# Two attentions of one program: scratch rows kept by head, fewer and later loads, another order at the second one's entry

## The reference, cut to what matters

```
x = ln(x + attention0(x))   # 16 heads of 8, softmax(q k / sqrt(8) - |i - j|), causal
x = ln(x + experts(x))      # 8 experts, each token to the one of its largest logit
x = ln(x + attention1(x))   # 16 heads of 64, rms norm on q and k, bias -(i - j) * omega * softplus(k . u), causal
x = ln(x + ffn(x))          # five linear maps of 128 to 512 to 512 to 512 to 128 with gates
```

## Time and profile before

| | us |
|---|---|
| median of 3 runs | 2205.83 |
| lowest, highest | 2204.8, 2212.89 |
| profiled execution | 2213.37 |
| its span, first to last instruction | 2211.6 |
| TensorE busy | 2041.5 (92%) |
| VectorE busy | 1389.9 (63%) |
| ScalarE busy | 1146.0 (52%) |

### The profile page before, as it was taken

The page is one execution under the profiler, slowest core; times in us unless marked ns, Lnnn a source line. Parts: engine busy times, 40 slices in busy tenths (PEclk is TensorE's granted clock), DMA queues, the critical chain, the costliest instruction groups (busy, mean ns, idle before and its releaser), DMA issues.

```text
span 2211.6 us, 37667 instructions
## 1 busy us (share of the span) xinstructions
PE 2041.5 (92%) x13392; PEld 1231.1 (56%) x13392; DVE 1389.9 (63%) x3316; ACT 1146.0 (52%) x1859; POOL 839.6 (38%) x544
## 2 busy tenths in 40 slices
PE   5799999998487988896999999999999999999998
PEld 3355455554476544454566666666666665656644
DVE  4788888883632787874677777777777764333311
ACT  2366666666344676782455555555555552232232
POOL 5000000001501445442577777777777772000000
PEclk8799999999589999995899999999999999999999
DMA  5233333113165689897477677767776697433300
GB/s 177 104 128 133 134 130 119 59 54 98 65 188 151 187 268 338 270 287 181 105 180 180 154 177 180 182 161 173 178 182 166 168 223 211 110 86 86 91 5 10
DMA packets 260313, 336.09 MB, mean 152 GB/s; under 512 B 22732, under 2 KB 181756, under 8 KB 259720
## 3 DMA queue, kind: packets, MB, share of 16 engines
q1 hardware_dynamic: 244824, 305.82, 51.6%
q0 software_dynamic: 7664, 24.39, 3.1%
q10 hardware_dynamic: 7640, 3.48, 0.6%
HBM read 193.69 MB, written 122.62 MB: 143 GB/s over the span
## 4 chain that ended last, share of the span: by engine, by line
PE 49%; DMA 2%; SPq 2%; DVE 0%; ACT 0%; issue 0%; DVEq 0%
PE ps L959 11%; PE ps L1296 10%; PE ps L910 7%; PE ps L941 6%; PE ps L942 6%; PE ps L1247 2%; PE ps L947 1%; PE ps L1307 1%; PE ps L922 1%; PE ps L1284 1%; PE ps L1285 1%; SPq L1171 1%; DMA a1QA<-a1QB 1%; DMA a1FQ<-s_q 1%; DMA s_y<-a1raw 0%; DMA fyb<-s_y 0%
## 5 line engine op out<-in xcount | busy, mean ns | idle before, releaser
L1132 POOL TENSOR_TENSOR a1sum<-a1sum,a1prob 128x1024 f32<-128x1024 f32 (+3 forms) x256 | 461.3, 1802 | 101.7 <-ACT a1prob L1075 69.7
L1075 ACT ACTIVATE a1prob<-ps 128x512 f32<-128x512 f32 (+2 forms) x640 | 322.7, 555 | 239.1 <-PE ps L947 206.3
L480 DVE TENSOR_REDUCE a0grid<-ps 128x8 f32<-128x1024 f32 x288 | 346.6, 1222 | 99.4 <-PE ps L350 48.8
L581 ACT ACTIVATE a0prob<-ps 128x1024 f32<-128x1024 f32 x288 | 291.3, 1027 | 159.0 <-PE ps L376 89.2
L1011 DVE CUSTOM_DVE_ANT_0 ps<-ps,c_mask_ij 128x128 f32<-128x128 f32 x496 | 264.6, 551 | 92.0 <-issue 87.7
L959 PE MATMUL ps<-a1prob,a1V 128*64 128x512 f32 (+3 forms) x1536 | 275.5, 501 | 4.9 <-ACT a1prob L1075 4.9
L941 PE MATMUL ps<-a1QA,a1KA 69*128 69x512 f32 (+3 forms) x768 | 272.3, 362 | 4.0 <-DMA a1QA<-a1neg 4.0
L942 PE MATMUL ps<-a1QB,a1KB 128*128 128x512 f32 (+3 forms) x768 | 264.9, 353 | 0.0
L910 PE MATMUL ps<-a1KA,a1QA 68*128 68x128 f32 x744 | 229.4, 385 | 5.0 <-DMA a1KA<-s_g 4.3
L959 PEld LDWEIGHTS ps<-a1prob,a1V 128*64 128x64 f32 x1536 | 103.3, 139 | 174.4 <-issue 140.2
L1014 DVE TENSOR_REDUCE a1mx<-ps 128x1 f32<-128x320 f32 x248 | 146.0, 589 | 60.0 <-PE ps L910 57.2
(11 more groups left out here) (269 smaller groups left out, 3191.7 us busy)
## 6 DMA issues: line engine op xcount, KB each, us to landing
a1FQ<-s_q SPq DMA_DIRECT2D x128, 256.0 KB, 7.8
a1KB<-s_k SPq DMA_DIRECT2D x128, 256.0 KB, 8.6
s_xs<-c_zero POOLq DMA_DIRECT2D x19, 1024.0 KB, 8.9
s_q<-mqkT SPq DMA_DIRECT2D x32, 512.0 KB, 4.0
s_v<-mv SPq DMA_DIRECT2D x32, 512.0 KB, 5.8
s_k<-a1KH SPq DMA_DIRECT2D x32, 512.0 KB, 4.9
s_k<-a1KL SPq DMA_DIRECT2D x32, 512.0 KB, 5.9
a1KA<-s_k SPq DMA_DIRECT2D x64, 256.0 KB
```

The costliest lines, as they stand in the source:

```text
L480: dve.tensor_reduce(grid[g % 2][:, :, a:b + 1:b - a], banks(("max", k)), axis=AX.X, op=ALU.max).then_inc(s1_free, 1)
L581: act.activation(prob[:, :, a:b + 1:b - a, :], banks(("exp", q)), ACT.Exp).then_inc(p_full, 1)
L1075: act.activation(weights_of(g, u)[:, group[0]:group[-1] + 1, off:BANK], both(e, u, group), ACT.Exp).then_inc(weighed, 1)
L1132: pool.tensor_tensor(t[:, :, off:BANK], t[:, :, off:BANK], weights_of(g, u)[:, :, off:BANK], ALU.add).then_inc(summed, 1)
```

## The change

1. The scratch s_q0, s_k0 becomes [384, tokens], a head's 24 rows together and in the order in which the tiles want them. `store` writes a part once for each of its three places: six transfers of 256 KB per chunk instead of four.
2. `still` then issues one transfer of 48 rows per half, `moving` one of 24 rows per head: 6 instead of 16 for `load_first` and for `load_second`. `part` goes.
3. SP also issues the first BK; ScalarE's wait and its eight issues go.
4. `load_second(1)` is issued behind the first row of maxima (and behind `load_first(2)`), not behind chunk 5.
5. Entry of the second attention: slopes first, V by itself and later (`load_v`); pair 1's maxima from unit 4 instead of 2; its turn at unit 10 instead of 9 and its row behind unit 11 instead of 10; the splits of pair 2 behind units 4 and 6 instead of 0 and 3, the first of its two `lower` at unit 8 instead of 4.
6. End of the middle part: VectorE takes the last gates behind 6 of the 24 maxima instead of 12; the two transposes are listed behind maxima 7 and 8 (counted from 0).

```diff
-        N_LOAD = 16 * 4 * H
+        N_LOAD, N_STORE = 16 * (PAIR + H), 16 * 6
...
         def still(engine, buf, name, g, done):
 
+            b, k = divmod(g, per)
+            for m in range(PAIR):
+                row, to, n = 3 * dim * (k * H + m * PAIR), base_of(m) + FIRST, 3 * dim * PAIR
+                engine.dma_start(buf[to:to + n, :].bitcast(F32), scr[name][row:row + n, b * seq:(b + 1) * seq]).then_inc(done, 16)
+
+        def moving(engine, buf, name, g, done):
+
+            b, k = divmod(g, per)
             for h in range(H):
-                part(engine, buf, name, g, h, done)
...
+                row, to, n = 3 * dim * (k * H + h), base_of(h // PAIR) + FIRST + 3 * (h % PAIR) * dim, 3 * dim
+                engine.dma_start(buf[to:to + n, h % PAIR, :].bitcast(F32), scr[name][row:row + n, b * seq:(b + 1) * seq]).then_inc(done, 16)
...
-                for r, part in enumerate((high, low)):
-                    nc.sync.dma_start(scr[name][r, :, c * CHUNK:(c + 1) * CHUNK], part[c % PARTS3][:, n, :].bitcast(F32)).then_inc(stored[c % PARTS3], 16)
+                rows_of = scr[name].rearrange("(h s d) n -> h s d n", s=3, d=dim)
+                for s, part in enumerate(((high, high, low), (high, low, high))[n]):
+                    nc.sync.dma_start(rows_of[:, s, :, c * CHUNK:(c + 1) * CHUNK], part[c % PARTS3][:, n, :].bitcast(F32)).then_inc(stored[c % PARTS3], 16)
...
             batch_stored(sp, 0)
+            sp.wait_ge(cleared_first, 1)
             still(sp, Q[0], "q0", 0, loaded1[0])
+            moving(sp, BK[0], "k0", 0, loaded1[0])
...
-                if c == 5:
-                    sp.wait_ge(cleared, 3)
-                    load_second(sp, 1)
...
-                if 0 < g and g + 1 < GROUPS:
-                    sp.wait_ge(s2_full, NU * g)
+                if g + 1 < GROUPS:
+                    if g > 0:
+                        sp.wait_ge(s2_full, NU * g)
+                    else:
+                        sp.wait_ge(cleared, 3)
                     load_second(sp, g + 1)
...
-            act.wait_ge(cleared_first, 1)
-            batch_stored(act, 0)
-            moving(act, BK[0], "k0", 0, loaded1[0])
...
-    share0 = ([0, 0, 2, 3, 3, 4, 4, 4, 4, 0, 0, 0], [0, 0, 0, 0, 0, 0, 0, 0, 0, 3, 3, 3])
+    share0 = ([0, 0, 0, 0, 4, 5, 5, 5, 5, 0, 0, 0], [0, 0, 0, 0, 0, 0, 0, 0, 0, 3, 3, 3])
...
-            return [("turn", 1, 0)] + found if u == TURN + 1 else found
+            return [("turn", 1, 0)] + found if u == TURN + 2 else found
...
+            load_e(1)
             for h in range(2):
                 copy_high(1, h)
                 load_a(1, h)
-            load_e(1)
             for k in range(PARTS):
                 load_f(2, k)
+            load_v(1)
+            load_e(2)
             for h in range(2):
                 load_a(2, h)
-            load_e(2)
+            load_v(2)
             for k in range(N_K):
                 load_b(2, k)
...
-                    if u == TILES and g + 2 < G:
+                    if u == (TILES if g > 0 else TURN) and g + 2 < G:
                         lower(g + 2, 0)
...
-                    if g + 2 < G and u in (0, 3):
-                        split(g + 2, (0, 3).index(u))
+
+                    behind = (0, 3) if g > 0 else (4, 6)
+                    if g + 2 < G and u in behind:
+                        split(g + 2, behind.index(u))
...
-                    if u == (TURN if g > 0 else TURN + 2) and g + 1 < G:
+                    if u == (TURN if g > 0 else TURN + 3) and g + 1 < G:
                         row(g + 1)
...
+        AHEAD = 6
...
-            here += [("max", k, 0) for k in range(NM // 2)] if n == LAST else []
-            here += [("aug", c, 0) for c in turn_gates.get(n, ())]
-            here += [("max", k, 0) for k in range(NM // 2, NM)] + [("turn", 0, 0)] if n == LAST else []
+            here += [("max", k, 0) for k in range(AHEAD + 2)] if n == LAST else []
+            for k, c in enumerate(turn_gates.get(n, ())):
+                here += [("aug", c, 0)] + ([("max", AHEAD + 2 + k, 0)] if n == LAST else [])
+            here += [("max", k, 0) for k in range(AHEAD + 2 + len(turn_gates[n]), NM)] + [("turn", 0, 0)] if n == LAST else []
```

More of the change, by code:

```diff
@@ L151, in batch_stored @@
             for c in range(b * seq // CHUNK, (b + 1) * seq // CHUNK):
-                engine.wait_ge(stored[c % PARTS3], 16 * 4 * (c // PARTS3 + 1))
+                engine.wait_ge(stored[c % PARTS3], N_STORE * (c // PARTS3 + 1))
         def load_first(engine, g):
@@ L168, in still @@
         def still(engine, buf, name, g, done):
-            for h in range(H):
-                part(engine, buf, name, g, h, done)
-        def moving(engine, buf, name, g, done):
-            for h in range(H):
-                part(engine, buf[:, h % PAIR, :], name, g, h, done)
-        def part(engine, buf, name, g, h, done):
-            b, m = divmod(g, per)
-            row, to = (m * H + h) * dim, base_of(h // PAIR) + FIRST + 3 * (h % PAIR) * dim
-            for r, n in PARTS[name]:
-                engine.dma_start(buf[to + r * dim:to + (r + n) * dim, :].bitcast(F32), scr[name][0:n, row:row + dim, b * seq:(b + 1) * seq]).then_inc(done, 16)
-        PARTS = {"q0": ((0, 1), (1, 2)), "k0": ((0, 2), (2, 1))}
+            b, k = divmod(g, per)
[4 more added lines that the diff above has]
+            b, k = divmod(g, per)
+            for h in range(H):
+                row, to, n = 3 * dim * (k * H + h), base_of(h // PAIR) + FIRST + 3 * (h % PAIR) * dim, 3 * dim
+                engine.dma_start(buf[to:to + n, h % PAIR, :].bitcast(F32), scr[name][row:row + n, b * seq:(b + 1) * seq]).then_inc(done, 16)
         def load_x(part):
@@ L576, in exponentials @@
                     for r in range(PARTS3):
-                        act.wait_ge(stored[r], 16 * 4 * len(range(r, chunks, PARTS3)))
+                        act.wait_ge(stored[r], N_STORE * len(range(r, chunks, PARTS3)))
                 if g > 0:
@@ L602, in drain @@
                 if c >= PARTS3:
-                    act.wait_ge(stored[c % PARTS3], 16 * 4 * (c // PARTS3))
+                    act.wait_ge(stored[c % PARTS3], N_STORE * (c // PARTS3))
                 act.activation(high[c % PARTS3][:, i, :], product_bank(n), ACT.Identity, bias=(bq, bk)[i][:, 0:1]).then_inc(high_full, 1)
@@ L810, in load_e, with load_v @@
             nc.sync.dma_start(KA[b][EXT:EXT + 4, :, :].bitcast(F32), slopes).then_inc(loaded_e[b], 16)
+        def load_v(x):
+            b, (n, m) = x % NB, divmod(x, PAIRS)
+            if x >= NB:
+                nc.sync.wait_ge(valued, unit(x - NB, NU - 1) + 1)
             nc.sync.dma_start(V[b][:, :, :], scr["v1"][n * S:n * S + S, m * P:m * P + P].rearrange("(t p) n -> p t n", p=P)).then_inc(loaded_v[b], 16)
@@ L864, in sync_program @@
                         load_e(g + 2)
+                        load_v(g + 2)
                         for h in range(2):
@@ L2360, in vector_last @@
                 if n == LAST:
-                    first_maxima(range(NM // 2))
+                    first_maxima(range(AHEAD))
                 for late in (2, 3):
@@ L2364, in vector_last @@
                         gates_b(event_of[EVENTS[n - late][0]])
-            first_maxima(range(NM // 2, NM))
+            first_maxima(range(AHEAD, NM))
             first_row()
@@ L2511, in scratch @@
         return nc.dram_tensor(name, shape, F32, kind="Internal").ap()
-    scr = {"q0": scratch("s_q0", [2, P, tokens]), "k0": scratch("s_k0", [2, P, tokens]),
+    scr = {"q0": scratch("s_q0", [3 * P, tokens]), "k0": scratch("s_k0", [3 * P, tokens]),
            "x2": scratch("s_x2", [tokens, P]), "ku": scratch("s_ku", [H1, DIM1]),
```

## The result

| | before | after |
|---|---|---|
| device time, median of 4 runs each | 2209.36 us | 2179.0 us |
| lowest to highest | 2204.8 to 2215.85 | 2177.36 to 2184.79 |
| profiled execution, and its span | 2213.37, 2211.6 | 2184.79, 2183.0 |
| mean granted clock of TensorE | 0.952 | 0.962 |

The ratio is 0.9865 with an interval of 0.983 to 0.990. The forecast was 2177.5 us (2164 to 2193). Between the two profiled executions lie 28.6 us, where the sum of the steps was 28.3.

The account below looks back on a forecast made before the run. TensorE was taken as full in the steady stretches, leaving gains at the two entries, held by loads and waits. Terms 6.8 + 5.4 + 3 + 0.6 + 12.5 = 28.3 us off the 2205.83 median gave 2177.5 us, range 2164 to 2193.

Parts of the forecast that it names:

- A: First entry: fewer, taller loads for the first group bring first maxima at 30.4 instead of 37.2, 6.8 us.
- the page's rule: First group's loads: a transfer uses the most engines up to 16 dividing both sides' outermost dimension; same 30.4 us.
- B: First row of maxima: second group's last loads go behind it, first scores at 83.6 instead of 89.0, 5.4 us.
- C: First scores: TensorE's upper clock level back 5.5 us behind them instead of 12.7; half of 7.2 won, 3 us.
- the sign that asked for the upper level: First entry: the upper clock level would be back within 10 us of the first scores.
- D: End of the middle: gates after 6 instead of 12 maxima cut VectorE's idling for the transposes, 0.6 us.
- E: Second entry: both TensorE holes go, pair 1's scores start at 1060.7 instead of 1073.8, 12.5 us.
- rival 3: First attention's stores: more of them, in scattered strips, run slowly and delay the first exponential; slower, 2273 us, chance 0.05.
- Rivals 1 and 2: Only the second entry pays, 2191 us, chance 0.11; only the first entry pays, 2190 us, chance 0.10.

Follow-up runs that it names:

- rows_apart: The changed kernel with one row left free behind each head's 24 rows in the scratch; 2182.34 us, ratio 0.9919.
- first_only: The kernel before with only the first attention's edits (neighbouring rows, fewer loads, second group's last loads behind the row); 2193.65 us, ratio 0.9948.
- row_behind_loads: The changed kernel with the second group's last loads ahead of the first row of maxima again; 2181.13 us, ratio 0.9899.
- fill_scores: The changed kernel with idle TensorE products added between the last drains and the first values of the first attention; 2175.92 us, ratio 0.9892.
- second_only: The kernel before with only the edits of the middle's end (gates) and of the second entry; 2195.43 us, ratio 0.9971.

## Why the prediction was right, and where it was not

**A, first maxima: 6.8 us forecast, 5.8 measured** (eight traces with the new loads, neighbouring rows and no added products in front: 31.15 to 32.10). Right in mechanism. The terms were off, in part against each other. The loads were issued in 2.5 us, not 3.5; but they began at 25.03 instead of 24.6, and landed 3.9 us behind the last issue instead of 2.3. I had taken the median landing of a row of 16 partitions for loads of 96 and 192 KB. The sum also left out that SP issues chunk 2's stores from 27.54 on: between 26 and 31 us DMA moved 1.2 MB, of which the loads are 786 KB. How much these stores delay the loads no run shows. The prediction took height and count for the cause of the low rate, and beside it the page's rule; rows_apart speaks for the rule, and shows that height and count alone give nothing.

**B, first scores: 5.4 us forecast, 7.5 measured** (51.8 less 44.3). 6.1 of it is the wait for the row (8.9 us from its issue to the scores before, 2.8 after). The other 1.4 are not the change's own: the distance is 44.2 to 44.3 in the six traces without added products whose clock came back 4.9 to 5.3 us behind the first maxima, and 45.6 to 45.8 in the three without a wait for the row where it took 9.7 to 10.2. Both first_only and row_behind_loads have the new loads and are of this second sort. The step was right on the wait and wrong on the cause: the prediction gave it to the order, but the tall loads of A had removed it already (row_behind_loads). Had I priced the second group's loads at the new rate, 786 KB at 236 GB/s or 3.3 us, the order would have been worth nothing behind A.

**C, clock: 3 us forecast, 0.5 measured.** This step failed, and with it the sign that asked for the upper level within 10 us of the first scores. From the first scores to the upper level it was 12.7 us before and 12.2 after. The step assumed that the restart at 77.84 in the old frame would count. It is the one at 70.70 in the new frame, and the level came back 17.2 us behind it. TensorE is held by VectorE before and behind that restart (70.00:72.00 above with 1.30 of 2 us busy, and 0.43 us ahead of the first scores); that this is the reason is likely, not shown. The price was too high as well: in fill_scores, with the level up throughout, only 2 us more come, net of the products' own time.

**D, gates: 0.6 us forecast, 0.7 measured.** From the first of pair 0's maxima to the entry it is 25.2 to 25.5 us in three traces without the edit, 24.4 to 25.2 in eleven with it, means 25.41 and 24.72. VectorE now idles 1.04 and 1.18 us while the transposes are due, where I had 0.95 twice, instead of 2.49 at once. No run changes the gates alone, and the two ranges all but touch.

**E, second entry: 12.5 us forecast, 12.5 in the two profiles, 12.3 by the means** of three traces without (47.9 to 55.0) and seven with the edits (38.0 to 42.5). Taken one against one, these traces give anything from 5.4 to 17.0, and second_only's whole time says 8.4, so the agreement to a tenth is luck. That the holes go, and that the splits carry the gain, is shown; the inside of the sum was less right. I had VectorE and the row as the chain up to pair 1's scores. The row was issued 37.2 us behind the entry, 2.9 earlier than I had it, and nobody waits for it: what ends last are TensorE's own values at the lower level (4.54 us at 1042.53). From the entry to there TensorE waits 1.0 us in all for VectorE, beside the 2.45 for the copy. The hole for pair 2's copy (2.45 us here, present in four of seven traces) was missing in the list of what is late next, though the prediction walked along SP's queue: it asked when each transfer is issued, not how many bytes lie ahead of it.

**The stores** did not bite (rival 3): 289 to 355 GB/s at a share of 0.91 to 1.02 between 14 and 24 us. Rivals 1 and 2 fell with second_only and first_only: in the traces each keeps its own part.

The sum of A, B, D and E in the profile is 5.8 + 7.5 + 0.7 + 12.5 = 26.5. C's half microsecond lies in the stretch from the first scores to the last stage, which is 0.3 us shorter (904.6 and 904.3), and the rest to 28.6 lies in stretches that the change leaves alone: from the first to the last row of maxima of the second attention it is 742.2 us before and 739.7 after. That the total came within 0.3 us is therefore partly luck: A and C were too high, B too low, and one execution of the changed kernel differs from the next by over 3 us at the entry alone. In the sum itself, half of C's 7.2 us is 3.6 and was entered as 3, and the exponential ahead of E's row has no term.

## What to carry to other kernels

When a load is slow, look at how its rows lie before counting transfers: loads of two times 24 rows with a gap began at 16 to 25 GB/s where 48 neighbouring rows began at 205. Ask of a short transfer that others wait for how many bytes are queued ahead of it, and price two edits that cure the same wait together, not one by one. And of an entry behind a slow phase take several traces before a gain of a few us is believed.

## What was not expected of the hardware

After the second entry, with the same work in the same order, the granted clock came back to 2.4 GHz after 38.6, 37.3 and 23.3 us in the three kernels without the edits, and after 3.7 to 10.4 us in the seven with them. Pair 1's scores moved by 7 us among the former and by 4.5 among the latter, and an early return is no gain by itself: TensorE then runs into the copy and loses the level again. The same shows behind the first maxima: back after 5.3 us in one execution, after 10.2 in first_only. The Trainium skill, "TensorE: Matmul & The Clock Gate", Part 1, calls this ramp run-variable. The traces agree, and the 4.5 and 7 us are more than all of D. Besides, the first attention's steady groups and the middle took 919 to 924 us from first scores to entry in the second set and 922 to 933 in the other two, in kernels that differ nowhere in that stretch but in the first few units. What sets it is open. The chip alone does not: the second and the third set ran on one and the same.
